# Moving the projection, second norm and routing of seven blocks into the attention's steps

## The reference

```
x = x + attention(layernorm(x), ctx, ctx, mask) @ W_out.T
h = layernorm(x)
q = tanh(h @ proj_w.T / 0.3);  logits = -(6 - q @ anchors.T) / 2 / temp
weights = softmax over the two largest of six logits
x = x + sum over those two experts e of weights[e] * (gelu(h @ w1[e]) @ w2[e])
```

## Time and profile before

| | us |
|---|---|
| median of 3 runs | 753.84 (751.01 to 757.17) |
| the profiled execution | 750.03 |
| its span, first to last instruction | 748.3 |
| attention until PE's last product with the values | 0 to 229.6 |
| middle, PE's first projection to PE's first expert matmul | 234.9 to 409.2 |
| experts and tail | 409.2 to 748.3 |

### The profile page before, as it was taken

One profiled execution on the slowest core, in us unless ns is written; L12 is line 12 of the kernel. 1 busy time (PEld: TensorE's weight loads), 2 busy tenths in 40 slices (PEclk: granted clock), 3 DMA queues, 4 the chain that ended last, 5 costly groups with the idle time before them and its releaser, 6 DMA issues.

```text
span 748.3 us, 15304 instructions
## 1 busy us (share of the span) xinstructions
PE 618.3 (83%) x4628; PEld 471.2 (63%) x4629; DVE 454.8 (61%) x972; ACT 323.4 (43%) x616; POOL 283.7 (38%) x414
## 2 busy tenths in 40 slices
PE   5989999999986988999853779999999999998000
PEld 3765555555523766776643768999999888887000
DVE  4857777776644648778762445555555667766465
ACT  4547767777674355545331223333333333332000
POOL 5425545554353247776674200000001222322674
PEclk9779999999998999999955798999999999999555
DMA  5311222212313686999737435665565888887686
GB/s 172 98 33 67 87 94 93 89 68 69 131 72 140 220 289 236 307 337 349 287 151 263 164 133 191 196 194 181 190 195 180 275 291 281 272 277 252 211 277 230
DMA packets 71529, 142.93 MB, mean 191 GB/s; under 512 B 8742, under 2 KB 11814, under 8 KB 71468
## 3 DMA queue, kind: packets, MB, share of 16 engines
q1 hardware_dynamic: 61228, 108.58, 43.1%
q0 software_dynamic: 10240, 33.56, 13.7%
HBM read 77.63 MB, written 64.49 MB: 190 GB/s over the span
## 4 chain that ended last, share of the span: by engine, by line
PE 46%; issue 16%; DMA 9%; DVE 9%; POOL 8%; SPq 4%; ACT 4%; another core or an unknown queue 2%; DVEq 1%; POOLq 0%; ACTq 0%
PE ps L1359 6%; DMA y_d<-ysb 6%; PE ps L1372 4%; PE ps L1421 3%; PE ps L1522 3%; PE ps L1523 3%; PE ps L1524 3%; PE ps L1543 3%; PE ps L1544 3%; PE ps L1545 3%; PE ps L1511 2%; PE ps L1392 2%; POOL yg L730 2%; PE ps L1438 2%
## 5 line engine op out<-in xcount | busy, mean ns | idle before, releaser
L730 POOL DMA_INDIRECT yg<-y_d,sidx x64 | 64.5, 1008 | 256.7 <-DVE wst L1211 222.8
L975 DVE TENSOR_REDUCE nmax<-ps 128x4 f32<-128x512 f32 x128 | 82.3, 687 | 54.0 <-PE ps L1359 54.0
L1522 PE MATMUL ps<-w1H,xgH 128*128 x296 | 91.4, 309 | 3.0 <-DVE xgL L1232 2.9
L893 ACT ACTIVATE xgH<-ps 128x512 fp32r<-128x512 f32 x74 | 44.3, 599 | 110.2 <-PE ps L1511 97.6
L791 ACT ACTIVATE prob<-ps 128x512 f32<-128x512 f32 x128 | 66.1, 602 | 48.6 <-PE ps L1375 48.6
L1524 PE MATMUL ps<-w1L,xgH 128*128 x296 | 85.0, 287 | 0.0
L1523 PE MATMUL ps<-w1H,xgL 128*128 x296 | 84.9, 287 | 0.0
L1359 PEld LDWEIGHTS ps<-kfT,qT 32*128 32x128 f32 x1024 | 68.2, 198 | 18.6 <-issue 9.5
L1359 PE MATMUL ps<-kfT,qT 32*128 32x128 f32 x1024 | 75.3, 290 | 2.8 <-DVE nmax L975 2.3
L1245 DVE COPY ysb<-ps 128x512 f32<-128x512 f32 x74 | 51.1, 690 | 43.3 <-PE ps L1545 23.4
L710 POOL DMA_INDIRECT xs_d<-x,place_now x64 | 63.7, 996 | 29.7 <-issue 20.5
(11 more groups left out here) (193 smaller groups left out, 1297.3 us busy)
## 6 DMA issues: line engine op xcount, KB each, us to landing
xg<-xs_d SPq DMA_DIRECT2D x74, 256.0 KB, 3.1
y_d<-ysb SPq DMA_DIRECT2D x74, 256.0 KB
xin<-in_x SPq DMA_DIRECT2D x32, 256.0 KB, 2.7
att_d<-atT SPq DMA_DIRECT2D x32, 256.0 KB, 2.0
atL<-att_d SPq DMA_DIRECT2D x16, 512.0 KB
x<-in_x SPq DMA_DIRECT2D x32, 256.0 KB
x_d<-x SPq DMA_DIRECT2D x32, 256.0 KB
x2t<-x_d SPq DMA_DIRECT2D x16, 256.0 KB, 2.7
```

Source lines behind the costliest of these rows:

```text
L730: nc.gpsimd.indirect_dma_start(yg[:, k, z, :], None, y_d[b], bass.IndirectOffsetOnAxis(ap=sidx[:, k, z:z + 1], axis=0))\
L975: nc.vector.tensor_reduce(nmax[:, n % 2, :, g * hpg + h], ps[:, token_bank(v, h), :].rearrange("p (t k) -> p t k", t=4), axis=AX.X, op=ALU ...
L1522: mm(o, xgH[:, p, c, :], w1h[:, cols], start=(c == 0), stop=False)
```

## The change

Steps of the attention go on to `S_LAST = 44`. From step `L_MID = 17` on, step s holds a quarter of what was a round of the middle: with `i, q = (s - 17) // 4, (s - 17) % 4` it projects tile q of block i, adds its residual, transposes a normalised tile of block i-1 (from step 22), and, by q, a piece of the routing of block i-2 (q = 1, 2, 3) and two scatters of block i-3. That is done for blocks 0 to 6. The projection's output goes to PSUM bank 3, the transposed rows to bank 2 and the router's numbers to bank 1, banks that the scores by key use as well; so PE waits for all four exponentials of the step ahead of the projection, and the scores by key of the next step wait until those banks are read. `atT` is no longer written to DRAM: ACT copies it to `atH` and POOL, which was not in this before, takes the remainder `atL`, one unit at a time. The middle's loop now runs only for i = 7 to 10, and all twelve weight pieces are in it: `W_AT` is (7, 7, 7, 7, 8, 8, 8, 8, 9, 9, 10, 10).

```diff
-    att_d = dram("att_d", [nblk, kchunks, P, 4 * P], F32)
+        INSIDE, I_OUT, I_T2, I_Z = nblk - 1, 3, 2, 1
...
+        L_SPLIT, L_MID = L_DIV + 1, L_DIV + 5
+        L_ROWS, L_T2 = L_MID - 2, 1
+        S_LAST = L_MID + 4 * INSIDE - 1
...
-        W_AT = (0, 1, 1, 1, 2, 2, 2, 3, 4, 5, 6, 7)
+        W_AT = (7, 7, 7, 7, 8, 8, 8, 8, 9, 9, 10, 10)
         def middle_loop(eng, body):
-            for i in range(nblk + 3):
+            for i in range(INSIDE, nblk + 3):
                 body(i)
...  POOL, in a step
+                i, q = quarter(s)
+                if q == 0:
+                    row_factors(i - 1)
...
+                u = s - L_SPLIT
+                if live(u, ntile):
+                    n, g = unit(u)
+                    pool.wait_ge(at_done, u + 1)
+                    pool.wait_ge(atH_done, u + 1)
+                    after(pool, out_ready, 4 * (n - 1))
+                    nc.gpsimd.tensor_tensor(atL[:, n % 2, g, :], atT[:, u % 2, :], atH[:, n % 2, g, :], ALU.subtract)\
+                      .then_inc(atL_done, 1)
+                i, q = quarter(s)
+                scatter(i - 3, q)
...  POOL, in the middle
             def middle(i):
+                row_factors(i - 1)
+                for t in range(4):
+                    scatter(i - 3, t)
                 for e, z, j in weights_at(i):
...  ACT, in a step
+                w = s - L_MID - 4
+                if live(w, ntile):
+                    normalise(w // 4, w % 4)
...
+                    nc.scalar.activation(atH[:, n % 2, g, :], atT[:, u % 2, :], ACT.Copy).then_inc(atH_done, 1)
+                w, count = rows_turned(s)
+                for z in range(count):
+                    if live(w + z, ntile):
+                        rows_out((w + z) // 4, (w + z) % 4)
+                if q == 1:
+                    logits_part(i - 2)
+                if q == 2:
+                    squash(i - 2)
+                if q == 3:
+                    exponentials(i - 2)
...  PE, ahead of the scores by key
+                after(pe, t2_done, rows_turned(v + L_KEY)[0])
+                after(pe, add_done, v + L_KEY - L_MID)
...  PE, in a step, ahead of the second half of the scores by token
+                i, q = quarter(s)
+                if i >= 0:
+                    if live(k, ntile):
+                        pe.wait_ge(exp_done, hpg * (k + 1))
+                    project(i, q)
+                w, count = rows_turned(s)
+                for z in range(count):
+                    if live(w + z, ntile):
+                        rows_transposed((w + z) // 4, (w + z) % 4)
```

More of the change, by code:

```diff
@@ L485, in middle @@
                           .then_inc(wr_in[j % 4], 16)
[L486 to L496, removed]
+                for t in range(4):
+                    store_rows(i, t)
+            sp.wait_ge(atL_done, ntile)
             middle_loop(sp, middle)
@@ L688, in middle @@
             def middle(i):
[L689 to L711, removed]
-                                x2[:, n % 4, t, :], None).then_inc(scattered[n % 2][t], 16)
+                row_factors(i - 1)
+                for t in range(4):
+                    scatter(i - 3, t)
                 for e, z, j in weights_at(i):
@@ L877, in middle @@
+                for t in range(4):
+                    rows_out(i - 1, t)
                 for e, z, j in weights_at(i):
@@ new lines, in _, with middle @@
+            attention_loop(attention)
+            def middle(i):
+                residual(i, 0)
+                n = i - 2
+                if live(n, nblk):
+                    router_logits(n)
+                for t in range(1, 4):
+                    residual(i, t)
+                moments(i)
+                if live(n, nblk):
+                    places(n)
+                    shares(n)
+                if i == blk_per_batch + 3:
+                    rows_of_tiles(0)
+                    table(0)
+                if i == blk_per_batch + 4:
+                    rows_of_tokens(0)
@@ new lines, in rows_transposed @@
+            def rows_transposed(n, t):
+                if live(n, nblk):
+                    pe.wait_ge(xn2_done, 4 * n + t + 1)
+                    if n + 1 < INSIDE:
+                        after(pe, t2_done, 4 * n + t)
+                    else:
+                        pe.wait_ge(mx_done, hpg * ntile)
+                        after(pe, t2_done, 4 * n + t - 1)
+                    for c in range(kchunks):
+                        last = nc.tensor.transpose(ps[:, t2_bank(n, t), c * P:(c + 1) * P], x2[:, n % 4, t, c * P:(c + 1) * P],
+                                                   ident[:])
+                    last.then_inc(t2_ready, 1)
@@ new lines, in logits_part @@
+            def logits_part(n):
+                if live(n, nblk):
+                    pe.wait_ge(t2_done, 4 * n + 4)
+                    after(pe, zp_done, n)
+                    if n + 2 == INSIDE:
+                        pe.wait_ge(newton_done, ntile)
+                        pe.wait_ge(raw_done, ntile)
+                    for c in range(kchunks):
+                        last = mm(ps[c * HD:(c + 1) * HD, zp_bank(n), :], projT[:, c, :], x2T[:, :, c, :], start=True, stop=True)
+                    last.then_inc(zp_ready, 1)
@@ L1453, in middle @@
[L1453 to L1470 removed]
+            def middle(i):
+                logits_part(i - 2)
+                project(i, 0)
+                logits(i - 2)
@@ L1484, in middle @@
+                prefix(i - 2)
                 project(i, 3)
```

395 lines of the change are left out of this document (207 added, 188 removed).

## The result

The changed kernel takes 777.04 us (median of 4 runs, 773.5 to 778.65), against 752.42 of the kernel before beside it (749.11 to 757.17, 4 runs): ratio 1.032 with an interval of 1.025 to 1.039. Timed a second time, with the experiments: 778.13 against 755.29, ratio 1.032, interval 1.025 to 1.038. The profiled execution took 773.5 us, its span is 771.7; before it was 748.3.

What follows compares the result with a forecast made beforehand. PE bounds the attention, then ACT's table loads from step 28, then GpSimd's queue before the experts. Attention's end 351.4, entry 428.0, plus 342.0 gives span 770.0, 21.7 more; on the median's scale 775 us, range 758 to 798.

Steps and rivals of the forecast that it cites:

- A: When the attention with its new work ends: 351.4 us, of which 22 us are waits.
- B: From the attention's end until PE may enter the experts at 428.0: GpSimd's queue of remainders and scatters, 75.6 us.
- A, by PE alone: PE's work from step 17 to the attention's end, old plus added: 242.7 us, ending at 329.3.
- A, the waits: Attention steps with new work: PE waits for ACT's table loads and for GpSimd, 22 us in all.
- ScalarE sets the pace of these steps: From step 28, two table loads make ACT's chain 10.3 to 10.4 us, over PE's 9.16 a step.
- VectorE I cost at nothing: Attention steps: VectorE's work, 30 us for four steps of over 40, delays nobody and covers the router's chain.
- 342.0, which the change leaves as they are: From PE's entry into the experts' stage to the span's end: 342.0 us, same as before.
- Nothing else is late: Middle: casts, piece loads and last block's routing (done about 45 us in, scatters at 60) do not delay GpSimd's queue.
- The waits were not hidden: Rival, attention: table loads fall into idle time and GpSimd keeps up; 753 to 764 us, chance 0.16.
- the faster rival: Middle: GpSimd's queue does not hold PE at the end, scatters about 0.5 us each; 718 to 738 us, chance 0.04.
- The longer table switch: Rival, attention: each switch holds ACT 2.66 us, fifteen steps 2.3 to 2.8 longer; 810 to 815 us, chance 0.05.
- Contention: Rival: operations take longer where VectorE and GpSimd are both full, adding 10 to 25 us; chance 0.13.

Runs made afterwards that it cites:

- both edits: Changed kernel with weight remainders on VectorE, table set preloaded behind each tanh, and router's logits ahead of the maxima at q = 3: 743.05 us, ratio to before 0.984.
- e2: Changed kernel with the twelve weight-piece remainders moved from GpSimd's queue to VectorE's: 750.93 us, ratio to the kernel before 1.022.
- the preload: ACT's table set reloaded behind each tanh; added to the changed kernel with remainders on VectorE and router's logits early: 753.2 us without it, 743.05 with it.
- e1: Changed kernel with only ACT's table set preloaded in each step with q = 2, loads 33 to 13: 763.05 us, ratio to the kernel before 1.037.

## Why the prediction was right, and where it was right by luck

The forecast was 775 us, measured 777; the sum was A 351.4 + B 76.6 + 342.0 = 770.0 of span, measured 356.5 + 80.0 + 335.2 = 771.7. Three terms were off by 5.1, 3.4 and -6.8, and cancel.

- **A, by PE alone: right.** 242.7 us of work and 22.1 of waits were forecast from step 17 on; the window 85.29 to 356.50 has 247.6 busy and 23.6 idle. Steps 17 to 28 took 103.1, forecast 113.8 less 10.5 for step 28, 103.3. Steps 28 to 40 took 136.0, forecast 134.8. The last four steps and the tail took 32.2, forecast 26.7; PE is idle 7.1 of them, one wait of 2.9 for `newton` in it, at a clock of 0.90.
- **A, the waits: the right sum from half the cause.** "ScalarE sets the pace of these steps" was one gate of two. The step that failed is "VectorE I cost at nothing", with the router's chain as its cover: by busy time it had 10 us to spare in four steps, but the chain hangs on when it starts and on GpSimd, which held single operations. Steps 32 and 36, with q = 3, took 12.2 and 11.9, forecast 10.4 and 10.1; steps 33 and 37 behind them 9.9 and 10.7, forecast 11.7 and 11.5, perhaps since a late step gives GpSimd time to catch up. That these errors cancel, and the sum comes out within 1.2 us, is luck. The stall for the maxima's split, forecast at 1.3 to 3.8 us in each of steps 29, 33 and 37, was 1.9 us in two waits. It took both edits to get 10.9 us back. (104.6 us over 25 steps are 4.2 a step and not 4.1, which changes nothing of this.)
- **B: right in its mechanism, short by 3.4.** It was GpSimd's queue to the end, as e2 shows by taking the remainders out of it. Counted from GpSimd's own end of the attention it was short by 7.0 (82.6 us, forecast 75.6), and 3.6 of these lie ahead of A's end, since GpSimd ended 2.6 us before PE and not 1.0 after it. From GpSimd's last scatter of the attention at 353.9 (forecast 352.4) come 2.2 us of wait for VectorE's `mv`, then 5.1 for the first rounded weights where I had taken 1, and 1.2 from the last remainder to PE; the twelve pieces took 28.2, forecast 30.1. "PE then idle for about 50 us in front of its first expert transposes" was 48 us of the whole middle, and 23.6 in one piece at its end.
- **"342.0, which the change leaves as they are": wrong.** Nothing in the experts' code changed, but what ran beside its first tile did: eight scatters and their transfers were gone, and the first result came 6.7 us sooner. The traces tie the two together by their order only; through which wait the scatters cost the time was not shown. Without this -6.8 the sum would have been 8.5 us short, and it is luck that the three terms cancel to 1.7.
- **"Nothing else is late": nearly.** Block 6's `pslot` on VectorE was held 9.88 us by four remainders, and its scatters started only 0.8 us late for it, as they stood behind the same remainders; that of the last block, block 7, took 0.21.
- **The rivals.** The waits were not hidden. The scatters cost 1.27 each in a row, as the earlier trace rows had it, so the faster rival's point of 0.5 was far off. The longer table switch: the load measured 1.283 us thirty times, and the operation behind it starts 0.02 us after its end. The Trainium skill, "ScalarE: Activation LUTs", section "What ACT_TABLE_LOAD costs", states a drain behind it; no row here shows one. Its rule in "Table sets: the hidden batching unit", to group calls by set, is borne out here: the preload is that, and with the second gate open it is worth 10.4 us in steps 28 to 40 (136.0 to 125.6).
  Contention, given 0.13, was there in another form than the forecast's: not longer operations all round, but single ones held.

## What to carry to other kernels

Work that moves into another stage takes its queue with it: count what every in-order engine has to finish before the next stage may start, and put what gates it ahead of what gates nobody, or on another engine. When a wait has two gates of like length, taking one away measures as nothing; try the two together before calling either harmless. Busy time tells whether an engine keeps up over a block, not whether a chain on it ends in time; follow the chain from what releases it.

## What was not expected of the hardware

- A short VectorE operation can be held while GpSimd runs subtractions back to back. The timeline of the changed kernel:

```profile
395.29 9.88 DVE L1071 TENSOR_TENSOR pslot<-pick,slot 128x48 f32<-128x48 f32 x1
...
395.86 2.36 POOL L740 TENSOR_TENSOR w1L<-w1L,w1H 128x1024 fp32r<-128x1024 f32 x1
...
402.76 2.33 POOL L740 TENSOR_TENSOR w2L<-w2L,w2H 128x1024 fp32r<-128x1024 f32 x1
```

  Its row ends with GpSimd's fourth subtraction and begins 0.57 us ahead of the first one. The same line takes 0.21 us at 413.72, beside scatters, and lasted 1.35 at 248.38 beside `atT`. In another place `wsel` and `pslot` were held 2.35 and 2.40, one subtraction each (378.41 and 380.69), and in e1 `place_now`, with one input tile, for 9.74. The Trainium skill, "GPSIMD Engine Reference", section "Key points", says that the two engines share their SBUF interfaces, with contention for VectorE instructions with two SBUF inputs or in a 2-port mode. The rows of `pslot`, `wsel` and `wgt`, with two inputs, agree, and give the length: up to the whole run of four subtractions. Whether `place_now` and `dot`, with one, ran in such a mode no row shows.
- The kernel before takes 736 us on two chips and 751 to 755 on the others, while versions of the changed kernel kept their stage lengths within a few us on all of them.
- TensorE's clock fell to 0.50 for some microseconds behind some of PE's waits and not behind others, in the same kernel at the same place (1.87 and 1.86 us). The 984 or 985 groups of matmuls of steps 28 to 40 took 119.1 to 127.0 us, a spread that goes with the granted clock (1.00 to 0.94) and is larger than what either edit moved by itself.
